# A sparse group's sixteen products handed out over the group's items, and its addition later

## The reference

```python
src_h = h[src] @ W_msg.T + b_msg
emb = edge_embed[jnp.clip(edge_type, 0, NUM_EDGE_TYPES)]
messages = jax.ops.segment_sum(src_h + emb, dst, num_segments=num_nodes)
h_new = _gru_cell(messages, h[:num_nodes], W_ih, W_hh, b_ih, b_hh)
x = _layernorm(x + h_new)
```

## Time and profile before

| | |
|---|---|
| Median of three runs | 1253.09 us (1248.27 to 1254.03) |
| The profiled execution, time | 1256.97 us |
| The profiled execution, span | 1255.1 us |
| PE, DVE, POOL busy | 1037.9, 859.2, 733.5 us |
| Granted TensorE clock, mean | 0.926 of full |

### The profile page before, as it was taken

How to read it: one execution, slowest core, us unless ns; L and a number is a source line. 1 busy time by engine, 2 the same in 40 slices (tenths; PEclk the granted TensorE clock), 3 DMA queues, 4 the chain that set the end, 5 groups by cost and what they waited for, 6 DMA issues and landing times.

```text
span 1255.1 us, 23526 instructions
## 1 busy us (share of the span) xinstructions
PE 1037.9 (83%) x8411; PEld 656.5 (52%) x8411; DVE 859.2 (68%) x2699; ACT 660.5 (53%) x1283; POOL 733.5 (58%) x779
## 2 busy tenths in 40 slices
PE   5456677888888988989889989889888888888884
PEld 2124354555555555556556656555555555555552
DVE  8413557677776877868777767777876777676644
ACT  4243404455655555656666656555655556554622
POOL 7725645665566666666666666566666666566640
PEclk9566568999999999999999999999998999999996
DMA  8529311222222322322333223223323233332321
GB/s 244 159 79 310 107 33 53 78 77 74 74 77 79 91 77 77 91 78 77 82 83 92 79 78 92 74 79 92 90 77 89 76 89 83 86 92 80 83 81 28
DMA packets 94565, 114.23 MB, mean 91 GB/s; under 512 B 19820, under 2 KB 80616, under 8 KB 94441
## 3 DMA queue, kind: packets, MB, share of 16 engines
q0 software_dynamic: 35264, 73.19, 21.8%
q1 hardware_dynamic: 57320, 37.79, 10.2%
q10 hardware_dynamic: 1856, 1.66, 0.5%
HBM read 96.56 MB, written 16.00 MB: 90 GB/s over the span
## 4 chain that ended last, share of the span: by engine, by line
PE 64%; issue 10%; DVE 9%; ACT 7%; another core or an unknown queue 7%; DMA 1%; SPq 1%; DVEq 0%; ACTq 0%
PE psf L1097 28%; PE psb L1082 14%; PE pAB L1026 5%; PE psg L1065 4%; PE pAB L1040 4%; ACT mem L1213 3%; DVE ohl L868 2%; PE pAB L1043 2%; DVE ohk L862 2%; PE psg L1069 2%; PE psf L1102 1%; DMA arena<-in_x 1%; ACT mem L1153 1%; DVE ohk L865 1%
## 5 line engine op out<-in xcount | busy, mean ns | idle before, releaser
L604 POOL DMA_INDIRECT xg<-x_split,idx x648 | 616.1, 951 | 392.1 <-PE psg L1069 151.0
L1213 ACT CAST mem<-psb 128x432 f16<-128x432 f32 x896 | 426.7, 525 | 398.4 <-PE psb L1082 300.8
L1097 PE MATMUL psf<-mem 128*128 128x384 bf16 (+1 forms) x2744 | 618.4, 330 | 13.6 <-issue 6.8
L1082 PE MATMUL psb<-ohk,ohl 128*128 128x108 bf16 (+3 forms) x1865 | 421.6, 264 | 97.9 <-issue 57.4
L862 DVE TENSOR_TENSOR ohk<-table_bank,prm 128x392 bf16<-128x392 f16 (+3 forms) x437 | 271.0, 620 | 108.6 <-PE psb L1082 69.1
L1097 PEld LDWEIGHTS psf<-mem 128*128 128x128 f16 (+1 forms) x2744 | 240.4, 99 | 131.3 <-issue 34.9
L1082 PEld LDWEIGHTS psb<-ohk,ohl 128*128 128x128 bf16 x1865 | 173.6, 100 | 251.3 <-issue 116.4
L868 DVE TENSOR_TENSOR ohl<-table_bank,prm 128x512 bf16<-128x512 f16 x437 | 180.8, 414 | 0.0
L891 DVE TENSOR_TENSOR mem<-mem,psg 128x136 f32 (+9 forms) x184 | 54.9, 298 | 168.4 <-remote 106.8
L604 POOL DMA_INDIRECT xg<-in_x,idx x88 | 84.2, 957 | 76.3 <-PE psg L1069 44.7
L865 DVE TENSOR_TENSOR ohk<-table_bank,sort 128x40 bf16<-128x40 f16 (+3 forms) x437 | 106.5, 244 | 0.0
(11 more groups left out here) (148 smaller groups left out, 808.4 us busy)
## 6 DMA issues: line engine op xcount, KB each, us to landing
xg<-x_split,idx POOLq DMA_INDIRECT x648
x_split<-mem SPq DMA_DIRECT2D x24, 384.0 KB
xb<-in_xT SPq DMA_DIRECT2D x49, 128.0 KB
arena<-in_x SPq DMA_DIRECT2D x24, 256.0 KB
arena<-in_xN SPq DMA_DIRECT2D x47, 128.0 KB
out<-spill SPq DMA_DIRECT2D x19, 128.0 KB
out<-arena SPq DMA_DIRECT2D x144, 8.0 KB
out<-arena SPq DMA_DIRECT2D x15, 128.0 KB
```

Of the source, the lines that this page charges most:

```text
L604: pool.indirect_dma_start(out=xg[:, p % RING, :] if split else xg32(p % RING), out_offset=None, in_=x_d if split else x, in_offset=bass.In ...
L1082: ins = pe.matmul(psb[:, bank % NB, held * HC:(held + m) * HC], ohl[:, e % KB, :], ohk[:, e % KB, d * HC:(d + m) * HC], start=(k == 0), st ...
L1097: pe.matmul(psf[:, 0:3 * H], Bb[q % 2][0:kk, HT + h, :], xs[0:kk, h, :, :].rearrange("p c f -> p (c f)"), start=(h == 0), stop=(h == HI - ...
L1213: act.copy(Bb[q % 2][:, :, n:n + MOST], psb[:, bank % NB, 0:MOST * HC].rearrange("p (d h) -> p h d", h=HC)).then_inc(S["s_eb"], 1)
```

## The change

The item `("G", g)` becomes four items `("G", g, 0)` to `("G", g, 3)`, one for each tile. Each holds the tile's three 16-bit products (or its one 32-bit product) and its edge-type product. The first keeps its place at the head of the group, and with it the waits for the one-hots and for the previous group's addition. The three others and GA are appended to the chunks at 0.15, 0.3, 0.45 and 0.62 of the group's chunks; groups of fewer than eight chunks have them in chunks 1 to 4, as far as there are so many. The addition to `s_used` stays on the last of the sixteen products. No product is added or left out.

```diff
-        chunks = [[("G", g)]]
+        chunks = [[("G", g, 0)]]
...
-        chunks[min(1, len(chunks) - 1)].append(("GA", g))
+        own = [("G", g, j) for j in range(1, G)] + [("GA", g)]
+        for j, it in enumerate(own):
+            at = (0.15, 0.3, 0.45, 0.62)[j]
+            chunks[min(1 + j, len(chunks) - 1) if len(chunks) < 8 else int(len(chunks) * at)].append(it)
...
-                        for j in range(G):
-                            p = g * G + j
-                            pe.wait_ge(s_g[p % RING], 16 * (p // RING + 1))
...
-                        for j in range(G):
-                            ins = pe.matmul(g2[:, 1, 0:w], tohb[:, g % AHEAD, j * ND2:j * ND2 + P], oh16[:, j, :], start=False,
-                                            stop=(j == G - 1), skip_group_check=True)
-                        ins.then_inc(S["s_used"], G)
+                        if j == 0:
+                            pe.wait_ge(S["s_oh"], g + 1)
+                            if g:
+                                pe.wait_ge(S["s_acc"], BEFORE[("GA", g - 1)] + 1)
+                        p = g * G + j
+                        pe.wait_ge(s_g[p % RING], 16 * (p // RING + 1))
...
+                        ins = pe.matmul(g2[:, 1, 0:w], tohb[:, g % AHEAD, j * ND2:j * ND2 + P], oh16[:, j, :], start=False,
+                                        stop=(j == G - 1), skip_group_check=True)
+                        if j == G - 1:
+                            ins.then_inc(S["s_used"], G)
```

More of the change, by code:

```diff
@@ L289, in updates_before @@
     for it in ITEMS:
-        if it[0] in ("G", "end"):
+        if it[0] == "G" and it[2] == 0 or it[0] == "end":
             start = n
@@ L913, in _ @@
                 for kind, back in (("G", AHEAD - 1), ("B", KB // OB - 1)):
-                    own = [it for it in ITEMS if it[0] == kind and (kind == "G" or it[1] % OB == 0)]
+                    own = [it for it in ITEMS if it[0] == kind and (it[2] == 0 if kind == "G" else it[1] % OB == 0)]
                     for a, it in enumerate(own):
@@ L918, in _ @@
                         else:
-                            ahead.setdefault(own[a - back] if a >= back else ("G", 0), []).append(it)
+                            ahead.setdefault(own[a - back] if a >= back else ("G", 0, 0), []).append(it)
                 for it in ahead[None]:
@@ L1050, in _ @@
                     if it[0] == "G":
-                        g = it[1]
+                        _, g, j = it
                         w = WG[g]
                         oh, oh16 = onehots(g)
-                        pe.wait_ge(S["s_oh"], g + 1)
-                        if g:
-                            pe.wait_ge(S["s_acc"], BEFORE[("GA", g - 1)] + 1)
-                        for j in range(G):
-                            p = g * G + j
-                            pe.wait_ge(s_g[p % RING], 16 * (p // RING + 1))
-                            if g < SWITCH:
-                                ins = pe.matmul(g2[:, 0, 0:w], xg32(p % RING), oh[:, j, :], start=(j == 0),
-                                                stop=(j == G - 1), skip_group_check=True)
[L1063 to L1067, removed]
@@ new lines, in _ @@
+                        p = g * G + j
+                        pe.wait_ge(s_g[p % RING], 16 * (p // RING + 1))
+                        if g < SWITCH:
+                            pe.matmul(g2[:, 0, 0:w], xg32(p % RING), oh[:, j, :], start=(j == 0),
+                                      stop=(j == G - 1), skip_group_check=True)
+                        else:
+                            for c in range(3):
+                                pe.matmul(g2[:, 0, 0:w], xg[:, p % RING, c * H:(c + 1) * H], oh16[:, j, :],
+                                          start=(j == 0 and c == 0), stop=(j == G - 1 and c == 2),
+                                          skip_group_check=True)
```

## The result

The changed kernel takes **1287.8 us** (median of 4 runs, 1284.28 to 1298.6) beside 1253.56 us for the kernel before (4 runs): a ratio of 1.0281 [1.023, 1.0332]. It is slower, as forecast, but by 34 us and not by 8: the time lies outside the range of 8 in 10. The profiled execution took 1290.26 us, its span is 1288.3 us at a mean clock of 0.927; before they were 1256.97 and 1255.1 us at 0.926.

What follows compares the result with a forecast made beforehand. The middle was taken as bound by POOL's gathers and late PE signals, 6.05 us a group, with PE some 2 us ahead. Terms 0 + 0 + 0 + 7 + 1 + 0 = +8 us on 1253 gave 1261 us; range 1238 to 1284 us.

Steps and rivals of the forecast that it cites:

- The direction and the place: Slower, in the middle (254 to 1200 us): POOL's long waits above 226.9 us, PE idle before a group's first product.
- The products: On PE, the same sixteen products in four pieces cost 0; at worst 0.48 us a group, within idle time.
- The floor of 6.05 us: In the middle, four gathers and the wait after them keep 6.05 us a group; only 25 us lie above it.
- the rival "faster": DVE builds one-hots instead of waiting, PE is late less often; half of 25 us goes, 1241 us, chance 0.23.
- DVE's early wait: DVE's 133.3 us of waits at the addition in the middle are slack and stay near that: gain 0.
- What lies between two posts: Post: a group's sixteenth product. Stages hh and su now share one interval in all 43 cases, making PE late: +7 us.
- The variant with a lead of 1 us: The same sum over intervals between posts, with PE only 1 us ahead of POOL's loop: +21 us.
- The wait for the previous addition: At a group's first product, PE waits for DVE's addition of the group before: +1 us, upper bound 18 us.
- The first groups: The first 23 groups, 100 to 254 us: change of 0, within -8 and +5 us.
- Much slower: The wait for the addition closes a loop in every group once PE's lead is used up: 1278 us, chance 0.11.
- The hold: PE's addition to s_used during POOL's gathers comes through only about 1 us after the run's last gather.

Runs made afterwards that it cites:

- r_late_first: Changed kernel with tiles at 0.3, 0.35, 0.4, 0.45 of the group, addition at 0.62, quick chip: 1084.33 us, 1.0006 of the kernel before.
- r_before: The kernel before, unchanged, profiled on a quick chip: 1084.39 us in one run.
- s_nogather: Kernel before without x_split gathers from tile 263 on, slower chip: 1161.25 us in one run, beside 1277.73 for the kernel before.
- e3_hh_early: Changed kernel with stage hh moved ahead of the fourth tile: 1284.84 us, 1.0217 of the kernel before.
- h3_late_first_hh: Changed kernel with tiles at 0.3 to 0.45 and hh ahead of the fourth tile, quick chip: 1086.75 us, 1.0018 of the kernel before.
- h1_late_first: Changed kernel with tiles at 0.3, 0.35, 0.4, 0.45, addition at 0.62, quick chip: 1087.19 us, 1.0021 of the kernel before.
- r_after: The changed kernel, unchanged, on a quick chip: 1111.06 us, 1.0249 of the kernel before.
- set 4: Four edited kernels beside the kernel before (1277.73 us) on one slower chip: 1161.25, 1274.94, 1291.86 and 1281.3 us.
- t_early: Changed kernel with tiles at 0, 0.05, 0.1, 0.15 and addition at 0.3, quick chip: 1105.41 us, 1.0203 of the kernel before.

## Why the prediction was wrong in size

*The direction and the place* were right: slower, in the middle, with the long waits of POOL above 226.9 us (260.7) and PE idle in front of a group's first product.

*The products, 0.* Right. r_late_first has the same pieces, and PE's busy time in its middle is 811.98 us for 621 gathers, 5.23 us a group for 5.24 in r_before.

*The floor of 6.05 us.* Right for this chip. The excess above it was put too high: by the prediction's own figures it is 946 - 153.25 x 6.05 = 19 us and not 25, which moves the rival "faster" by 3 us and the forecast not at all. After, runs of gathers that meet no late PE still start 6.1 us apart, here from 798.61 to 804.70; the next starts after a wait of 2.71 us:

```profile
798.61 0.95 POOL L607 DMA_INDIRECT xg<-x_split,idx  x1 [1.11 <-PE psg L1071]
...
804.70 0.94 POOL L607 DMA_INDIRECT xg<-x_split,idx  x1 [1.39 <-PE psg L1071]
...
812.11 0.94 POOL L607 DMA_INDIRECT xg<-x_split,idx  x1 [2.71 <-PE psg L1071]
```

That it is the gathers that set it was read from a rhythm before, and s_nogather has shown it on one chip of this kind. The page "Perfetto Trace Analysis" of the Trainium skill ("Tensor Engine Instruction (MATMUL, LD_WEIGHTS)") has the update pushed once PSUM has acknowledged; the quick chips agree (DVE's waits at the addition in r_before are 41.8 us for PE's products, and none "remote"). Here the update arrives late, and the trace doesn't tell whether it is pushed late or is long on its way.

*DVE's early wait, 0.* The gain was nothing, as put, but "at three fifths it is reached later, but the release comes later too", and with it waits that stay near 133 us, was wrong: 14.1 us are left. DVE doesn't stand at the addition any more since it gets there late. That was the sign of the step that failed.

*What lies between two posts, +7 us.* Not the cause. The reading of the list was right (all 43 pairs fall into one interval), the price wasn't borne out: e3_hh_early took the coincidence away and kept 2.2%, h3_late_first_hh changed nothing against h1_late_first. (The variant with a lead of 1 us adds up to 21.6 us, not 21.)

*The wait for the previous addition, +1 us.* **This step failed.** Put at 1 us, it measured 36.3 us of pauses in the profiled middle for 1.7 before, twice its upper bound of 18; the middle lost 47 us, 33 of it idle time of PE. r_after has 21.6 us for none, beside a loss of 26.7 us (spans 1109.3 and 1082.6). The step's reason was that PE "restarts at 737.25 for want of a bank anyway", from the earlier trace rows. But that row shows a product released at the head of a group and an addition that DVE was already standing at. In the new order `t2`, a clearing and a build stand in front of the addition, and the step gave them a sentence without a price. Priced as an estimate, with the durations of the timeline after: from the post a release up to 2.3 us later, a build of 0.36 + 0.19 + 0.41 us and the addition with its way to PE, 0.42 us (936.66 to 937.08), make 3.7 us in the plain case. PE has 0.55 of a group to the next first product, 2.5 us without stages. That is 1.2 us short where the release is held that long, and only stages, a turn or a pause of PE cover it. The bound of 18 us was taken from DVE's idle time, and no idle time bounds what a queue puts in front of one instruction.

*The clock, no term.* The sum had none. PE is busy 13.8 us longer with the same products in the middle, at a granted clock of 0.971 for 0.984, and in r_after 14.5 us longer at 0.988 for 1.000. This part of the loss stands beside the pauses. Whether the pauses bring the lower clock about was not tested.

*The first groups, 0.* A gain of 13.3 us up to group 23, beyond its bound of 8, at a clock of 0.80 for 0.75 from 100 to 254 us. It offset more than a quarter of the middle's loss. That the change brings it is not shown: on one chip group 23 begins at 232.1 us in s_nogather, whose first groups are those of the kernel before, and anywhere from 228.8 to 255.0 in the three others of set 4; on the quick chips the change moves it from 183.6 to 181.4.

*The rivals.* "Much slower" at 1278 us was this mechanism, "release, DVE's queue, first product, half a group, post". Its condition, a lead that is used up before the group's head, holds in 32 of some 145 groups, not in all. It came closest with a chance of 0.11, and for its sum it took 7 us from the term that proved wrong. The hold that I built it on isn't needed: r_after loses 2.5% without one.

## What to carry to other kernels

When an instruction that others wait for is moved later in an in-order queue, price what then stands in front of it, from the moment at which it could start to the waiter's turn: the waits for a row that looks idle today say nothing on it. A first product that waits for the bank of the group before holds up all of PE's queue, so look at the distance from the addition to the next such product. With 0.68 of a group the four pieces lost 0 to 0.2% on three chips, with 0.55 2.1%, with 0.38 2.5 and 2.8%. It is not all that counts: with 0.7, but the pieces at the group's head, t_early lost 2.0% without pauses. Time the kernel before again beside each set, since what bounds it may differ from chip to chip.

## What the runs showed of the hardware

The same kernel took 1252 to 1278 us on some chips and 1083 to 1085 us on others. Each chip was used in one set only, so that "the chip" may stand for something else that was the same throughout a set. Most of the difference goes with the gathers: leaving most of them out gave 116 us on a chip of the one kind and nothing on two of the other. Where they are left out, groups 66 to 177 take as long on both (605.3 and 605.2 us). What remains lies before group 66, where s_nogather still gathers: it begins at 502.6 us there and at 426.5 in r_before. On the quick kind POOL's row has no "remote" release; the gathers of r_before, 190 to 1040 us:

```profile
L604 POOL DMA_INDIRECT xg<-x_split,idx x623: 940/947/1196, 189.9 to 1037.8; - x156
  issue: 164.2, 539
  PE psg L1069: 93.1, 84
```

The instruction itself lasts as long on both kinds (947 and 949 ns). What differs is how late PE's signals arrive, by 2.4 us in the earlier trace rows. The updates of `s_used` in the traces show it group by group. From the start of the sixteenth product to its update it takes 1.53 us in the median in the kernel before (254 to 1200 us), and over 1 us in 105 of 153 groups. In r_before it takes 0.21 us in the median; there 10 of 154 read as over 1 us, but some updates are missing from the records (175 for 184 groups). In s_nogather, on a slow chip, it takes 1.94 us in the median from 254 to 380 us, and without gathers, from 503 to 1100 us, 0.22 us at most in 110 groups. So the hold needs both, such a chip and gathers under way. Why some chips do this is not known, and no run here could tell.

The late addition alone costs 0.9 to 1.0% on two chips of the slow kind and 4.0% on one of the quick kind. A reason that fits is that PE had slack at the floor there, and that its own work sets the pace here; this was not tested.
